# Loading the projection weights one phase ahead, with one staging tile for K and Q and half-width V loads, in a transformer layer on eight cores

## What is computed

```
x = layernorm(x + attention(x))        # x: 4 x 4096 x 2048 float32, 16 heads of 128
    qkv = x @ w_qkv.T + b_qkv;  q, k = rope(q), rope(k)
    att = softmax(causal(q k^T / sqrt(128)));  (att v) @ w_out.T + b_out
x = layernorm(x + ffn(x))
    W = (int32 weight - 128) * scale   # gate, up: 8192 x 2048; down: 2048 x 8192
    (silu(x Wg^T) * (x Wu^T)) Wd^T
```

## Time and profile before

| | us |
|---|---|
| median of 2 runs | 6263.97 |
| the two runs | 6125.63 and 6402.32 |
| profiled execution, own time | 5853.5 |
| profiled execution, span of the slowest core (core 5) | 5852.0 |
| span of the 8 cores in it | 5805.2 to 5852.0 |
| PE busy | 5016.7 (86%) |
| DVE, ACT, POOL busy | 1111.0, 1016.6, 371.5 |
| mean granted TensorE clock, core 5 | 0.943 |

### The profile page before, as it was taken

The page is one execution under the profiler, slowest core; times in us unless marked ns, Lnnn a source line. Parts: engine busy times, 40 slices in busy tenths (PEclk is TensorE's granted clock), DMA queues, the critical chain, the costliest instruction groups (busy, mean ns, idle before and its releaser), DMA issues. The chain is left out here.

```text
span 5852.0 us, 61112 instructions; the slowest of 8 cores (5805.2 to 5852.0 us)
## 1 busy us (share of the span) xinstructions
PE 5016.7 (86%) x24640; PEld 2256.9 (39%) x24640; DVE 1111.0 (19%) x1111; ACT 1016.6 (17%) x1174; POOL 371.5 (6%) x688
## 2 busy tenths in 40 slices
PE   3999294999788888846689999999999949898987
PEld 1444141444333333323334444444444414444433
DVE  1333031111000000013322222222222211111111
ACT  0111010000566666611200000000000000000001
POOL 1000100000000000000022112112112000000000
PEclk9999697999899999978899999999999979999998
DMA  9442715121211112052244224224224066768665
GB/s 161 99 99 71 131 42 112 67 81 53 76 46 56 44 46 63 27 121 94 84 70 78 47 49 78 47 49 76 49 48 76 21 125 166 175 196 199 184 216 193
DMA packets 306834, 543.19 MB, mean 93 GB/s; under 512 B 27904, under 2 KB 232832, under 8 KB 297856
## 3 DMA queue, kind: packets, MB, share of 16 engines
q1 hardware_dynamic: 176320, 378.75, 19.7%
q0 software_dynamic: 130240, 160.54, 18.7%
HBM read 565.46 MB, written 134.22 MB: 120 GB/s over the span
## 5 line engine op out<-in xcount | busy, mean ns | idle before, releaser
L952 PE MATMUL y2p<-wdm,hsb 128*128 128x512 bf16 x4096 | 934.9, 385 | 156.4 <-DMA wdm<-dwM 96.6
L801 PE MATMUL gps<-y1nfm,wg_sb 128*128 128x512 bf16 x4096 | 907.0, 380 | 19.9 <-DMA wu_sb<-uwT 19.9
L826 PE MATMUL ups<-y1nfm,wu_sb 128*128 128x512 bf16 x4096 | 904.9, 379 | 0.0
L952 PEld LDWEIGHTS y2p<-wdm,hsb 128*128 128x128 bf16 x4096 | 403.0, 99 | 661.8 <-issue 193.4
L500 ACT ACTIVATE ptq<-sps 128x1024 bf16<-128x1024 f32 (+7 forms) x768 | 589.5, 774 | 300.2 <-PE sps L440 222.1
L801 PEld LDWEIGHTS gps<-y1nfm,wg_sb 128*128 128x128 bf16 x4096 | 400.8, 98 | 505.4 <-issue 23.1
L826 PEld LDWEIGHTS ups<-y1nfm,wu_sb 128*128 128x128 bf16 x4096 | 401.2, 98 | 482.9
L232 PE MATMUL pkk<-xqk,wT1bk 128*128 128x512 bf16 x2048 | 456.9, 382 | 91.3 <-DMA xqk<-xbT 91.3
L349 PE MATMUL pv<-wvT,xst 128*128 128x512 bf16 x2048 | 443.6, 380 | 76.9 <-DMA wvT<-wvT_in 76.9
L470 PE MATMUL smtp<-ptq,allones 128*128 128x512 bf16 (+3 forms) x1280 | 373.8, 358 | 140.0 <-ACT ptq L500 132.0
L819 ACT ACTIVATE gsl<-tg,gsc_sb 128x1024 bf16<-128x1024 bf16 x128 | 146.9, 1148 | 1607.4 <-DVE tg L813 1607.4
(11 more groups left out here) (89 smaller groups left out, 2505.2 us busy)
## 6 DMA issues: line engine op xcount, KB each, us to landing
hsb<-h_sp SPq DMA_DIRECT2D x32, 4096.0 KB, 15.9
wg_sb<-gwT POOLq DMA_DIRECT2D x256, 128.0 KB, 7.6
wu_sb<-uwT POOLq DMA_DIRECT2D x256, 128.0 KB, 7.7
h_sp<-hst SPq DMA_DIRECT2D x256, 128.0 KB, 1.8
wdm<-dwM POOLq DMA_DIRECT2D x8, 4096.0 KB, 82.1
xqk<-xbT POOLq DMA_DIRECT2D x64, 256.0 KB, 22.3
x_bf<-xqk SPq DMA_DIRECT2D x64, 256.0 KB, 7.2
k_sp<-kstk SPq DMA_DIRECT2D x64, 256.0 KB, 3.3
```

The costliest lines, as they stand in the source:

```text
L801: E.matmul(gps[:, c:c + 512], wg_sb[buf][:, f, ici * 128:(ici + 1) * 128], y1nfm[:, f, th * 1024 + c:th * 1024 + c + 512], start=(f == 0), ...
L826: E.matmul(ups[:, c:c + 512], wu_sb[buf][:, f, ici * 128:(ici + 1) * 128], y1nfm[:, f, th * 1024 + c:th * 1024 + c + 512], start=(f == 0), ...
L952: E.matmul(y2p[tb4][:], hsb[hsl][:, i2, tb4 * 128:(tb4 + 1) * 128], wdm[wsl][:, i2, :], start=(hh == 0 and i2 == 0), stop=(hh == 1 and i2 ...
```

## The change

A pair of 8 MiB weight tiles `wpair` is allocated before the K phase and kept until V is done. The K weights go into the first. The Q weights go into the second, issued by POOL in the K phase right behind the first x group (`pre_emit`). The V weights go into the first again, issued in the Q phase right behind its first x group. `woT` and `y1nfm` are allocated before attention, and `woT` is loaded at the start of attention, behind the masks. To make room, `kst` becomes one tile, `v2` holds one head (1 MiB in pieces of 256 bytes, loaded at every head), and the unused `identf`, `gbias_sb`, `ubias_sb` go, with one transfer and two DVE operations.

```diff
-            wT = es.enter_context(nc.sbuf_tensor(f"wT1b{tag}", [128, 16, C], BF16))
-            kst = [es.enter_context(nc.sbuf_tensor(f"kst{tag}{i}", [128, 1024], BF16))
-                   for i in range(2)]
+            kst = [es.enter_context(nc.sbuf_tensor(f"kst{tag}0", [128, 1024], BF16))] * 2
-            for f in range(16):
-                wtw = sc.dma("g", f"wt{tag}", wT[:, f, :],
-                             wT_in[f * 128:(f + 1) * 128, :])
...
+                if qt == 0 and pre_emit is not None:
+                    pre_emit()
...
-                    sc.wait("s", f"kst{tag}{kb}", kst_free[kb])
+                    sc.wait("s", f"kst{tag}0", sc.cnt.get(f"kst{tag}0", 0))
...
+    wpair_cm = [nc.sbuf_tensor(f"wpair{i}", [128, 16, C], BF16) for i in range(2)]
+    wpair = [cm.__enter__() for cm in wpair_cm]
+    def load_wT(dst, src_ap, tag):
+        w = 0
+        for f in range(16):
+            w = sc.dma("g", f"wt{tag}", dst[:, f, :],
+                       src_ap[f * 128:(f + 1) * 128, :])
+        return w
+    wload_box = {}
+    wload_box['k'] = load_wT(wpair[0], wkT, 'k')
     if stop >= 3:
+        phase_proj_rope(wpair[0], wload_box['k'], bkr_sb, ckA_in, ckB_in, xbT,
+                        T, k_sp, 'k',
+                        pre_emit=lambda: wload_box.__setitem__(
+                            'q', load_wT(wpair[1], wqT, 'q')))
     if stop >= 4:
+        phase_proj_rope(wpair[1], wload_box.get('q', 0), bqr_sb, cqA_in, cqB_in,
+                        xownT, NTOK, q_sp, 'q',
+                        pre_emit=lambda: wload_box.__setitem__(
+                            'v', load_wT(wpair[0], wvT_in, 'v')))
...
-            for f in range(16):
-                wtw = sc.dma("g", "wtv", wvT[:, f, :],
-                             wvT_in[f * 128:(f + 1) * 128, :])
+            wvT = wpair[0]
+            wtw = wload_box.get('v', 0)
...
-            v2 = [es.enter_context(nc.sbuf_tensor(f"v2_{i}", [128, 32, 256], BF16))
+            v2 = [es.enter_context(nc.sbuf_tensor(f"v2_{i}", [128, 32, 128], BF16))
                   for i in range(2)]
             mkw = sc.dma("g", "mks", masksT[:], masksT_in)
+            for f in range(16):
+                sc.dma("g", "wto", woT[:, f, :], woT_in[f * 128:(f + 1) * 128, :])
...
-                if h % 2 == 0:
-                    vb2 = (h // 2) % 2
-                    sc.wait("y", "T", v2_free[vb2])
-                    vw_cur[0] = sc.dma("y", f"v2_{vb2}", v2[vb2][:],
-                                       [:, :, h * 128:(h + 2) * 128])
+                sc.wait("y", "T", v2_free[hb2])
+                vw_cur[hb2] = sc.dma("y", f"v2_{hb2}", v2[hb2][:],
+                                     [:, :, h * 128:(h + 1) * 128])
```

More of the change, by code:

```diff
@@ L144, in build_program @@
     ident = EO(nc.sbuf_tensor("ident", [128, 128], BF16))
-    identf = EO(nc.sbuf_tensor("identf", [128, 128], F32))
     m1 = EO(nc.sbuf_tensor("m1", [128, 64], BF16))
@@ L153, in build_program @@
     usc_sb = EO(nc.sbuf_tensor("usc_sb", [128, 64], F32))
-    gbias_sb = EO(nc.sbuf_tensor("gbias_sb", [128, 64], F32))
-    ubias_sb = EO(nc.sbuf_tensor("ubias_sb", [128, 64], F32))
     eps_sb = EO(nc.sbuf_tensor("eps_sb", [128, 1], F32))
@@ L159, in build_program @@
         sc.dma("g", "c0g", dst[:], src)
-    sc.dma("y", "c0y", identf[:], ident_in)
     for dst, src in ((bqr_sb, bq_r), (bkr_sb, bk_r), (gsc_sb, gsc_in),
@@ L167, in build_program @@
     sc.opn("v", lambda E: E.memset(allzeros[:], 0.0))
-    for dst, src in ((gbias_sb, gsc_sb), (ubias_sb, usc_sb)):
-        sc.opn("v", lambda E, d=dst, s=src: E.tensor_scalar_mul(d[:], s[:], -128.0))
     sc.op("v", "V", lambda E: E.memset(eps_sb[:], EPS))
@@ L172, in build_program, with phase_proj_rope @@
     sc.flush()
-    def phase_proj_rope(wT_in, b_sb, cA_in, cB_in, xT_in, ntok, dst_sp, tag):
+    def phase_proj_rope(wT, wtw, b_sb, cA_in, cB_in, xT_in, ntok, dst_sp, tag,
+                        pre_emit=None):
         es = ExitStack()
         with es:
-            wT = es.enter_context(nc.sbuf_tensor(f"wT1b{tag}", [128, 16, C], BF16))
             xq = [es.enter_context(nc.sbuf_tensor(f"xq{tag}{i}", [128, 16, 1024], BF16))
@@ L281, in stage_R @@
                     kst_free[kb] = sc.dma(
-                        "y", f"kst{tag}{kb}",
+                        "y", f"kst{tag}0",
                         dst_sp[hh, :, qt * 1024:(qt + 1) * 1024], kst[kb][:])
@@ L293, in phase_proj_rope @@
             sc.flush()
+    wpair_cm = [nc.sbuf_tensor(f"wpair{i}", [128, 16, C], BF16) for i in range(2)]
[8 more added lines that the diff above has]
+    wload_box['k'] = load_wT(wpair[0], wkT, 'k')
     if stop >= 3:
-        phase_proj_rope(wkT, bkr_sb, ckA_in, ckB_in, xbT, T, k_sp, 'k')
+        phase_proj_rope(wpair[0], wload_box['k'], bkr_sb, ckA_in, ckB_in, xbT,
+                        T, k_sp, 'k',
+                        pre_emit=lambda: wload_box.__setitem__(
+                            'q', load_wT(wpair[1], wqT, 'q')))
     if stop >= 4:
-        phase_proj_rope(wqT, bqr_sb, cqA_in, cqB_in, xownT, NTOK, q_sp, 'q')
+        phase_proj_rope(wpair[1], wload_box.get('q', 0), bqr_sb, cqA_in, cqB_in,
+                        xownT, NTOK, q_sp, 'q',
+                        pre_emit=lambda: wload_box.__setitem__(
+                            'v', load_wT(wpair[0], wvT_in, 'v')))
     def phase_vproj():
@@ L302, in phase_vproj @@
         with es:
-            wvT = es.enter_context(nc.sbuf_tensor("wvT", [128, 16, C], BF16))
+            wvT = wpair[0]
+            wtw = wload_box.get('v', 0)
             bv_bc = es.enter_context(nc.sbuf_tensor("bv_bc_sb", [128, C], F32))
             bvw = sc.dma("y", "bv", bv_bc[:], bv_bc_in)
-            for f in range(16):
-                wtw = sc.dma("g", "wtv", wvT[:, f, :],
-                             wvT_in[f * 128:(f + 1) * 128, :])
             xst = [es.enter_context(nc.sbuf_tensor(f"xst{i}", [128, 16, 512], BF16))
@@ L379, in build_program @@
         phase_vproj()
+    for cm in reversed(wpair_cm):
+        cm.__exit__(None, None, None)
+    y1nfm_cm = nc.sbuf_tensor("y1nfm", [128, 16, NTOK], BF16)
+    y1nfm = y1nfm_cm.__enter__()
+    woT_cm = nc.sbuf_tensor("woT", [128, 16, C], BF16)
+    woT = woT_cm.__enter__()
     def phase_attn():
@@ L413, in phase_attn @@
             spsrot = [0]
-            vw_cur = [0]
+            vw_cur = [0, 0]
             def stage_STAV(h, band, hb, kqw):
@@ L419, in stage_STAV @@
                 tmax = 16 * band + 16
-                hoff = (h % 2) * 128
-                vb2 = (h // 2) % 2
+                hoff = 0
+                vb2 = h % 2
                 qbase = band * 1024
@@ L490, in stage_STAV @@
                         sc.wait("t", "mks", mkw)
-                    if h % 2 == 0:
-                        sc.wait("t", f"v2_{vb2}", vw_cur[0])
+                    sc.wait("t", f"v2_{vb2}", vw_cur[vb2])
                 for t in range(tmax):
@@ L547, in head_loads @@
                 kqn = sc.dma("y", f"kq{hb2}", Qh[hb2][:], q_sp[h])
-                if h % 2 == 0:
-                    vb2 = (h // 2) % 2
-                    sc.wait("y", "T", v2_free[vb2])
-                    vw_cur[0] = sc.dma("y", f"v2_{vb2}", v2[vb2][:],
-                                       v_sp.rearrange("(tt p) d -> p tt d", p=128)
-                                       [:, :, h * 128:(h + 2) * 128])
+                sc.wait("y", "T", v2_free[hb2])
+                vw_cur[hb2] = sc.dma("y", f"v2_{hb2}", v2[hb2][:],
+                                     v_sp.rearrange("(tt p) d -> p tt d", p=128)
+                                     [:, :, h * 128:(h + 1) * 128])
                 return kqn
@@ L568, in build_program @@
         phase_attn()
-    y1nfm_cm = nc.sbuf_tensor("y1nfm", [128, 16, NTOK], BF16)
-    y1nfm = y1nfm_cm.__enter__()
     def phase_outproj():
@@ L575, in phase_outproj @@
         with es:
[L576 to L584, removed]
+            wtw = sc.cnt.get("wto", 0)
             bo_bc = es.enter_context(nc.sbuf_tensor("bo_bc_sb", [128, C], F32))
@@ L629, in phase_outproj @@
                         sc.wait("t", f"avs{abuf}", avw)
+                    if tb == 0 and fh == 0:
+                        sc.wait("t", "wto", wtw)
                     for d in range(16):
-                        if tb == 0 and d % 4 == 0:
-                            sc.wait("t", wtw_f[d][0], wtw_f[d][1])
                         for cpos in (0, 512):
@@ L737, in build_program @@
         phase_outproj()
+    woT_cm.__exit__(None, None, None)
     def phase_gateup():
```

## The result

| | before | changed |
|---|---|---|
| median over all runs, us | 5975.79 (10 runs) | 5878.02 (13 runs) |
| lowest run, us | 5845.63 | 5785.56 |
| profiled execution: span of the slowest core | 5852.0 | 5790.6 |
| profiled execution: median of the 8 cores' spans | 5825.2 | 5770.8 |
| PE busy in it | 5016.7 | 5014.1 |

A forecast was written before the change was run, and what follows sets the result against it. PE's waits after barriers, filled by loads, were taken to bound the kernel. Terms -57 -56 -50 +56 +46 +17 +3 gave -41 us, taken from the two-run median 6264 to 6223 us (chance 0.58), range 6060 to 6330.

The forecast's parts named there:

- Part 1: Gap ahead of the Q projection: without the weights x is loaded first and PE starts earlier, -57 us.
- Part 2: Gap ahead of V: x transfers with no weights beside them are issued and land sooner, -56 us.
- part 3: First wait of the output projection: `avs` reloads without `woT` beside it, -50 us.
- Part 4: Start of attention: head 0's V alternates packet for packet with `woT` and lands behind it, +56 us.
- Part 5: K's first group: Q weights delay the `x_bf` copies and the results behind them; one staging tile stalls PE, +46 us.
- Part 6: Q's first group: writes beside V weights and x loads slow the heads through one staging tile, +17 us.
- Part 7: Small things: slower PE restarts after idling, +3 us; per-head V loads hidden, removed `identf` and DVE operations taken as 0.
- Rival B: Start of attention: V's small pieces slip past `woT`, cost there about +6, sum -91 us, 6173 us; chance 0.13.
- Rival A: Attention, K and Q: all moved loads are hidden, -163 us, 6101 us; chance 0.14.
- Rival C: K and Q: ACT waits on the single staging tile beside cast loads; at 21 us landing 17 us slower, 6281; chance 0.15.

The follow-up runs named there:

- two_kst: Changed kernel with two staging tiles again, rotary tables held as bf16 and loaded by POOL; K phase 522.8 us against 536.4.
- room_only: Kernel before with only one staging tile and V loaded for one head at each head; ratio 0.9999 to the kernel before.
- both_moved: Changed kernel with Q weights behind K's last x group and output weights behind head 1's V load; ratio 0.9797 to the kernel before, median span 5699.3 us.
- wq_behind_x3: Changed kernel with the Q weights issued behind K's last (fourth) x group instead of the first; K phase 515.9 us against 536.4.
- wo_behind_v1: Changed kernel with output weights issued by POOL only once V of head 1 has landed; median span 5704.1 us against 5770.8.

## Why the prediction was right and wrong

**The time in microseconds was wrong, and by the level it was put on.** The changed kernel's median is 5878, the range on record began at 6060. The step that failed is "I take the difference over in microseconds: 6223", from the median of two runs, 6264. The profiled execution's own 5853.5 stood beside it, and the text took the 7% between them as given. Of the 26 later runs of the same kernel before, 11 lay at 5836 to 5860 and none below. The sum on the profiled execution's own time, 5812.5, lies 27 us above the lowest run of the changed kernel. With two runs 277 us apart and a profiled execution well below both, the kernel was known to reach the low level, and a range had to go down there. Where exactly the median of 13 runs falls is chance: 6 of them lie at 5786 to 5806, 6 at 6181 to 6578, and the 5878 alone between.

**The difference was forecast as -41 and is about -60 (-54 to -61 in the profiled executions; the two ratios give -65 and -83 on 5855).** The sign was right, the mechanisms of parts 1 to 5 were there, and the terms were off as follows. The gains of parts 1 to 3 were put 15 us too high and the costs of parts 4 to 6 some 33 too high. The two errors partly cancel, and that the sum came out only 16 us off its -44 is luck to that extent.

- *Part 1, ahead of Q:* -57 forecast, -48.9 measured. The x group took longer from issue to use, 643.09 to 681.34 on core 0, 38 us, where the sum had 30. The first of its 16 transfers took 9.7 us to land and the last landed 28.3 us behind that one (issued at 650.9, 30.2 us). So the packets' own 27 us were right, and the term that was too small is the "some 3" for what lies around them; the mechanism was right.
- *Part 2 and part 3:* -56 and -50 forecast, -52.8 and -45.9 measured. The wait of 23.4 us ahead of V and of 23.1 ahead of the output projection stood near 21 and 20 in the text.
- *Part 4, attention:* +56 forecast, +46.9 measured. V landed behind the weights, piece for piece. The wait itself was 74.8 on core 0 against 84 forecast, because 57 us for the weights and 7 for V were counted one after the other. The weights, with V's pieces among them, were down 53.5 us after the masks (1474.5 against 1421.0), where the sum had 61, and V was down 1.8 us later, where it had 3. Those 57 had been measured with 1 MiB of tables beside them, and the 439 small pieces took 8.0% of the engines' time against 92.3% (the queue counts above). Rival B, in which V overtakes, is refuted: V landed behind the last of the weights.
- *Part 5, K:* +46 forecast, +36.3 measured. The stall at R(3) was 28.75 us against 32.7, and its end was off by 2 us only (161.1 against 163.3). What follows it was put at 13 and was 5.7, since a write beside the x load needed 11.4 us once and then 7.8 and 8.4: 11.5 us a head was too slow a pace. The aside that two tiles would have waited two heads later was off: it is one head, since R(4) comes 7.57 us after R(3): 28.75 less 7.57 is 21.2, `two_kst` shows 19.1, and two heads would have made it 13.6.
- *Part 6, Q:* +17 forecast, +3.3 measured. This step failed. It stretched the landing time by the length of the neighbour's packets, to 15 us beside weights. The writes of the Q phase beside weights landed in 7.9 to 10.6 us, no later than beside x loads. At such a pace the slack of 13.2 us holds almost until the loads are over: the largest delay of an ACT copy was 12.9 us (749.94 against 699.19 + 5 x 7.57 = 737.0), and PE waited 0.9 us for ACT on this core, 4.0 on the worst.
- *Part 7:* the small V loads are hidden (`room_only`); the restart is seen in the granted clock of 0.93 in 161 to 200 (core 0), some 3 us of these 39 (an estimate), as much as the text had.

The four writes of part 6 beside weights, issued in 690 to 736 (the tile `q_sp`, core 0):

```profile
L68 SPq DMA_DIRECT2D q_sp<-kstq x4: 319/323/327, 700.3 to 730.7; - x4
DMA to landing us min/median/max: 7.9/9.5/10.6
```

Rival A, everything hidden, would have given -163. It is refuted in each of the two places, and `both_moved` shows how much of it was to be had by the place alone: some 70 of the 83 us that the two waits took. Rival C, slower by the single tile, is refuted by the landing times, all under its point of 16.5 us but that of the first write of K, behind the copies.

What was only argued: that the clock costs the 5 us in K of `wq_behind_x3` is worked out from the granted clock of one stretch. Why the first transfer of the x group ahead of Q takes 9.7 us to land was not tried.

## What to carry to other kernels

A load that is moved ahead leaves its old wait at once, but it costs in the new place whatever stands behind it there: list what the transfers of that stretch release, and put the load behind the last of them that an engine waits for. The same 8 MiB cost 47 us beside the first head's V and nothing behind the second head's. And when the runs shown lie far apart and above the profiled execution, let the range reach down to the profiled execution's level.

## What the runs showed of the hardware

The two queues, when both had work, took turns packet for packet on the DMA engines, whatever the sizes: 439 packets of 256 bytes against 439 of the weights, 388 of these of 4 KB, in 10 us. The counts alone would also fit turns of ten and ten. The times of the single packets in the trace settle it: in 1430 to 1440 a packet of the weights starts 2 to 5 ns before the end of 438 of V's 439 pieces, and another piece of V does so at 17% of them only, no more than at any other moment. The Trainium skill (DMA: Bandwidth & Descriptors, "Queues, rings and completion order") has them take turns by packets of about 9 to 17 descriptors. If a piece is a descriptor, the trace disagrees. The text on record also drew too much from that section when it let ten small pieces pass and hardly any of the weights': by the same section the weights' queue is drained in packets of that length too, and V would wait about as long as one for one. So small pieces beside a cast load move at the pace of the big ones: 4096 of 256 bytes took 69.4 us to land at head 0, and 16.9 at head 0 where the load came later (`wo_behind_v1`).

A single 256 KB write that was under way wholly beside a cast load landed in 7.5 to 12.2 us, whether the load's packets were 2 KB or 4 KB. Without a load most take 2.0 to 3.4.
